# Counting edges in a graph kernel: one-hots of two chunks in one comparison, a span of 24 targets per pair of chunks, 1200 columns of folding per group

## The chip, the cores and the metric

The kernel runs on one core of one Trainium2 chip. The metric is the device time of one execution in microseconds; the median of three runs before the change is 589.65 us (589.12 to 589.82). A profile is one execution recorded by the hardware profiler.

## The reference

Input is `x` (1024 nodes x 512), and 32768 edges `src`, `dst`, sorted by `dst`. Four layers follow each other, each with a residual and a layer norm:

```python
edge_index = jnp.stack([src, dst])
x = _layernorm(x + L0(x, edge_index, W0, b0))            # adj @ (x @ W0), symmetric 0/1 adjacency, normalised
x = _layernorm(x + L1(x, edge_index, W1, b1, W2, b2, W3, b3))   # three GCN convolutions with edge counts
x = _layernorm(x + L2(x, edge_index, Wq, bq, Wk, bk, Wv, bv))   # softmax((q k^T / sqrt d) masked by adj) @ v
x = _layernorm(x + L3(x, edge_index, V1, c1, V2, c2))    # two GCN convolutions, relu between
```

Every layer needs the edges as a dense 1024 x 1024 matrix: how many edges lead from source s to target d. The kernel calls it `count`; the change is wholly in how `count` is made.

## The kernel before, in words

**Counting.** The edges lie in 64 groups (`G`) of 512, a group in 4 chunks (`CPG`) of 128 edges, one edge per partition. A source s is split into low part `s % 128` and high part `s // 128` (8 values). For every chunk two one-hot matrices are made in bf16: `hot_lo` (128 edges x 128 low parts) and `hot_key` (128 edges x 320 keys). A key is the pair of high part (8) and distance of the target from the group's lowest target (`WIN` = 40): 8 x 40 = 320 (`KEYS`). One matmul per chunk, `hot_lo` as weights and `hot_key` as the moving operand (`chunk`, L527), adds the four chunks of a group in one PSUM bank; VectorE adds that bank to 40 columns of each of the 8 blocks of `count` (`add_window`, L1032), at a column that it reads into a register from `base_at` (`windows_at`, L1025, once for 8 groups). Edges are sorted by target, so 512 of them span few targets; how many rounds are needed to cover the widest group is computed on the chip (`rounds`, L1014). In this input the widest group spans 33 targets, so there is one round; pairs of chunks (256 edges) span 18 targets at most.

**Who makes the one-hots.** VectorE makes `hot_lo` of the first two chunks (`BY_DVE` = 2, L1020) and all four `hot_key` (L1022), each by a `tensor_scalar` that compares a 16-bit table of numbers with one fp32 scalar per partition. ScalarE makes `hot_lo` of the other two (L850, L854), and copies the results of the folding (below) out of PSUM. There are 4 slots; VectorE makes the one-hots of group g + 3 (`AHEAD`) before it adds the window of group g. Before an add it waits for two things: `win_summed` (the matmuls of this group) and `win_added` (its own add before). One loop body (`dve.Fori`, L1053) holds 8 groups.

**Folding.** Between groups TensorE is given other work: transposes and products of weights ("pieces", L446 to L509: `xw`, `m`, `u`, `tb`, `w12`, `bw`, `wf`, `g`). A written-out plan spreads them: each group gets a credit of `SHARE` = 1300 columns, and a piece of fp32 with 512 columns counts 1024. What the plan leaves over stands behind the loop: first `BEHIND`, then `REST`, whose first piece waits for `counted` (L454, the whole of `count` is done), and whose pieces stand two by two between the eight transposes of the 0/1 matrix (`turn_links`, L560, L574 to L581). Then come the last piece `g` (L489) and layer 0's aggregation (`rows_step`, L583, L599). With 1300 the plan puts 162 pieces along the loop and 14 behind it, with 1200 it puts 154 along and 22 behind.

**Behind the loop** VectorE makes `link` (L1075, 8 instructions), then one row block of `sym` after each transpose (L1080), with the low parts of the operands of layer 0 between them (`low`, L1066, L1084).

Each engine executes its queue in order. Instructions that only compute a register, load one (`TENSOR_LOAD`), branch or wait are executed by the engine's own sequencer, which can be some instructions ahead of the engine's datapath. The profile calls VectorE's sequencer DVEq.

Of the kernel before, what the change touches and what calls it, by code (L numbers as in the profile page):

```python
# [16 lines left out]
ALU = mybir.AluOpType  # L17
ACT = mybir.ActivationFunctionType
# [8 lines left out]
P = 128  # L27
# [4 lines left out]
CPG = 4  # L32
WIN = 40
BY_DVE = 2
EARLY = 24 * 128
SHARE = 1300
# [7 lines left out]
def gnn_kernel(nc, x, src, dst, w0, b0, w1, b1, w2, b2, w3, b3, wq, bq, wk, bk, wv, bv, v1, c1, v2, c2, out):  # L44
# [7 lines left out]
    KEYS = NB * WIN  # L52
    SCALE = float(D) ** -0.5
    assert N + 2 * WIN <= APART and NB * APART <= 32768
    assert D == 512 and NB == 2 * HALF and G % BODY == 0 and BODY % SLOTS == 0 and KEYS <= 512 and G <= P

    with ExitStack() as ctx:
# [24 lines left out]
        hot_lo = at("hot_lo", at_adj, [P, SLOTS * CPG, P], BF16)  # L82
        hot_key = at("hot_key", at_adj + SLOTS * CPG * P * 2, [P, SLOTS * CPG, KEYS], BF16)
# [41 lines left out]
        keyed = at("keyed", r3 + 2 * W, [P, 3, CPG * G], F32)  # L125
# [32 lines left out]
        col_key = sb("col_key", [P, KEYS], I16)  # L158
# [4 lines left out]
        group_lim = sb("group_lim", [G, 4], F32)  # L163
        group_dia = sb("group_dia", [G, 2, G], F32)
        group_row = sb("group_row", [P, 2, G], F32)
        base_at = sb("base_at", [1, G], I32)
# [40 lines left out]
        win_added = sem("win_added")  # L207
        counted = sem("counted")
# [158 lines left out]
        def _(pool):  # L367
# [17 lines left out]
            nc.gpsimd.iota(col_key[:], pattern=[[APART, NB], [1, WIN]], base=0, channel_multiplier=0,  # L385
# [59 lines left out]
        def _(pe):  # L445
# [78 lines left out]
            pe.matmul(bank[:, 0, 0:2 * G], ones[0:G, :], group_dia[:].rearrange("g a b -> g (a b)"),  # L524
                      start=True, stop=True).then_inc(rows_turned, 1)
# [21 lines left out]
            with pe.If(rounds > 1):  # L547
                with pe.Fori(1, rounds) as r:
                    with pe.Fori(0, G // BODY) as q:
                        for n in range(BODY):  # L550
                            pe.wait_ge(win_added, r * G + q * BODY + (n + 3 - SLOTS))
                            for c in range(CPG):
                                pe.wait_ge(hot_set, (r * G + q * BODY) * CPG + (n * CPG + c + 1))
                                if c == BY_DVE:
                                    pe.wait_ge(act_hot_set, r * G + q * BODY + (n + 1))
                                mm = chunk((n % SLOTS) * CPG + c, n % SLOTS, c)
# [261 lines left out]
        def _(act):  # L818
# [28 lines left out]
            def low_one_hots(g, slot, before):  # L847
# [6 lines left out]
                nc.scalar.activation(hot_lo[:, slot * CPG + BY_DVE:(slot + 1) * CPG, :], apart[:, slot % 2], ACT.Relu,  # L854
# [120 lines left out]
        def _(dve):  # L975
# [3 lines left out]
            def then(ins):  # L979
# [11 lines left out]
            V.tensor_reduce(group_lim[:, 0:1], edge_rows[:, 0, :], AX.X, ALU.min)  # L991
            then(V.tensor_reduce(group_lim[:, 1:2], edge_rows[:, 0, :], AX.X, ALU.max))
            V.tensor_scalar(key_rows[:, 2, :], edge_rows[:, 0, :], group_lim[:, 0:1], None,
                            ALU.subtract).then_inc(rows_set, 1)
            then(V.tensor_tensor(group_lim[:, 2:3], group_lim[:, 1:2], group_lim[:, 0:1], ALU.subtract))
            dve.wait_ge(const_set, 1)
            V.tensor_scalar(group_dia[:, 0, :], ident[0:G, 0:G], group_lim[:, 0:1], None, ALU.mult)
            V.tensor_scalar(group_dia[:, 1, :], ident[0:G, 0:G], group_lim[:, 2:3], None,
                            ALU.mult).then_inc(rows_set, 1)
# [4 lines left out]
            V.tensor_tensor(keyed[:, 1, :], bank[:, 3, 0:CPG * G], edge_key[:, 1, :], ALU.add).then_inc(win_added, 1)  # L1004
            dve.wait_ge(rows_turned, 4)
            V.tensor_copy(group_row[:].rearrange("p a g -> p (a g)"), bank[:, 0, 0:2 * G]).then_inc(win_added, 1)
# [4 lines left out]
            then(V.tensor_copy(flags[0:1, 0:1], rounds_f[0:1, ROUNDS + 1:ROUNDS + 2]))  # L1011
            V.memset(shift[:], 0.0).then_inc(rounds_set, 1)
# [12 lines left out]
            def windows_at(g):  # L1025

                _, values = nc.values_load_multi_w_load_instructions(
                    base_at[0:1, bass.ds(g, BODY)], engines=[mybir.EngineType.DVE], min_val=0, max_val=N,
                    skip_runtime_bounds_check_because="the table's entries are clamped to [0, N] when it is written")
                return values  # L1030

            def add_window(at_dst, seen, slot):  # L1032
# [3 lines left out]
                V.tensor_tensor(count[:, :, bass.ds(at_dst, WIN)],  # L1036
# [276 lines left out]
```

## Time and profile before

| | us |
|---|---|
| median of three runs | 589.65 |
| the profiled execution's own time | 589.9 |
| its span, first to last instruction | 587.6 |
| granted TensorE clock, mean | 0.999 of full |
| first one-hot to last window added | 11.4 to 122.85 |
| folding left over, transposes of the links, `g` | 122.8 to 142.1 |
| layers 0 to 3 | 142.1 to 587.6 |

PE is TensorE, PEld its weight loads, DVE VectorE, ACT ScalarE, POOL GpSimd. A row of a timeline gives start, duration, engine, line, operation and in brackets the idle time before it with what ended it; instructions of one kind that follow each other are merged (x3), and overlap a little, so from the start of one to the start of the next is what counts for a rate. An fp32 matmul appears as two records.

### The profile page before, as it was taken

How to read it: one execution, taken by the hardware profiler on the slowest of the kernel's cores; microseconds unless marked ns; L12 is line 12 of the kernel's file. 1: busy time of each engine (PE TensorE's matmuls, PEld its weight loads, DVE VectorE, ACT ScalarE, POOL GpSimd, SP SyncE). 2: the span in 40 equal slices, each digit the busy share in tenths (PEclk: the TensorE clock that was granted, in tenths of full speed). 3: DMA queues.
4: the chain of work that ended last, by engine and by line, in shares of the span. 5: the costliest groups of instructions: out<-in, count | busy, mean ns of one | idle time of the engine just before them, and what ended most of it. 6: DMA issues, size and time to landing. Idle time of an engine off the chain costs nothing.

```text
span 587.6 us, 6488 instructions
## 1 busy us (share of the span) xinstructions
PE 575.8 (98%) x2121; PEld 344.8 (59%) x2121; DVE 297.2 (51%) x821; ACT 176.6 (30%) x364; POOL 100.4 (17%) x112
## 2 busy tenths in 40 slices
PE   6999999999999999999999999999999999999996
PEld 4555655555788745888845444444445587458743
DVE  7999899948678034233591103333335430450065
ACT  5988689737011311110002011211114102110200
POOL 2000000017333500000170002033332170000011
PEclk9999999999999999999999999999999999999999
DMA  8624000000100000000040000000000000000012
GB/s 300 221 73 143 1 1 1 2 2 6 31 3 0 1 0 0 1 0 1 9 155 0 1 0 1 0 0 1 0 0 1 1 0 1 0 0 1 0 55 91
DMA packets 9429, 16.19 MB, mean 28 GB/s; under 512 B 1571, under 2 KB 1843, under 8 KB 9398
## 3 DMA queue, kind: packets, MB, share of 16 engines
q1 hardware_dynamic: 9398, 15.75, 8.0%
q8 instruction: 22, 0.36, 0.3%
q14 instruction: 9, 0.07, 0.0%
HBM read 13.64 MB, written 2.11 MB: 27 GB/s over the span
## 4 chain that ended last, share of the span: by engine, by line
PE 97%; DVE 1%; issue 1%; DMA 0%; POOL 0%; POOLq 0%; SPq 0%; DVEq 0%
PE bank L663 18%; PE bank L616 15%; PE bank L599 15%; PE bank L764 9%; PE bank L784 9%; PE bank L528 6%; PE bank L499 5%; PE bank L752 5%; PE bank L507 2%; PE bank L472 2%; PE bank L503 2%; PE bank L774 1%; PE bank L460 1%; PE bank L464 1%; PE bank L485 1%; PE bank L671 1%
## 5 line engine op out<-in xcount | busy, mean ns | idle before, releaser
L411 POOL TENSOR_TENSOR rstd<-veps,mhalf 128x1 f32<-128x1 f32 x32 | 23.5, 733 | 301.3 <-DVE veps L1097 298.5
L1022 DVE TENSOR_SCALAR hot_key<-col_key,keyed 128x320 bf16<-128x320 int16 x256 | 65.5, 299 | 0.0
L764 PE MATMUL bank<-xt,tt 128*128 128x512 f32 x128 | 56.1, 593 | 0.0
L784 PE MATMUL bank<-vv,probt 128*128 128x512 f32 x128 | 56.1, 592 | 0.0
L663 PE MATMUL bank<-v_sb,gt 128*128 128x512 f32 (+1 forms) x136 | 55.3, 567 | 0.0
L616 PE MATMUL bank<-adj,y_hi 128*128 128x512 f32 x128 | 51.8, 405 | 0.0
L616 PE MATMUL bank<-adj,y_lo 128*128 128x512 f32 x128 | 50.2, 392 | 0.0
L528 PEld LDWEIGHTS bank<-hot_key,hot_lo 128*128 128x128 bf16 x256 | 25.0, 98 | 38.8 <-DVE hot_key L1022 17.2
L528 PE MATMUL bank<-hot_key,hot_lo 128*128 128x320 bf16 x256 | 45.4, 300 | 0.0
L850 ACT ACTIVATE apart<-col_lo,edge_key 128x128 bf16<-128x128 int16 x128 | 43.8, 390 | 0.0
L1104 DVE SCALAR_TENSOR_TENSOR xs<-bank,dinv,xs 128x512 f32<-128x512 f32 x23 | 17.0, 748 | 52.0 <-PE bank L663 37.3
L663 PEld LDWEIGHTS bank<-v_sb,gt 128*128 128x128 f32 x136 | 25.9, 190 | 28.7 <-issue 27.7
L784 PEld LDWEIGHTS bank<-vv,probt 128*128 128x128 f32 x128 | 24.2, 190 | 29.6 <-issue 29.6
L764 PEld LDWEIGHTS bank<-xt,tt 128*128 128x128 f32 x128 | 23.9, 190 | 27.7 <-issue 27.7
L1211 DVE SCALAR_TENSOR_TENSOR score<-bank,rr,mask 128x1024 f32<-128x1024 f32 x8 | 10.3, 1283 | 55.5 <-PE bank L764 55.5
L1036 DVE TENSOR_TENSOR count<-bank,count 128x320 f32 x64 | 31.3, 488 | 7.1 <-PE bank L528 7.1
L1020 DVE TENSOR_SCALAR hot_lo<-col_lo,edge_key 128x128 bf16<-128x128 int16 x128 | 31.9, 250 | 2.5 <-issue 2.4
L854 ACT ACTIVATE hot_lo<-apart,ones 128x256 bf16<-128x256 bf16 x64 | 32.5, 508 | 2.1
L499 PE MATMUL bank<-w_sb,x0t 128*128 128x512 f32 x64 | 32.6, 607 | 0.0
L431 POOL TENSOR_SCALAR mask<-count 128x1024 bf16<-128x1024 uint16 x8 | 22.5, 2810 | 52.4 <-DVE peak L1219 52.3
L959 ACT COPY probt<-bank 128x1024 f32<-128x1024 f32 x8 | 8.1, 1013 | 72.7 <-PE bank L774 72.7
L616 PEld LDWEIGHTS bank<-adj,y_hi 128*128 128x128 f32 x128 | 24.0, 188 | 6.6 <-issue 0.5
(176 smaller groups left out, 943.4 us busy)
## 6 DMA issues: line engine op xcount, KB each, us to landing
w_sb<-in_L_gnn_W_dram SPq DMA_DIRECT2D x3, 1024.0 KB, 5.5
xs<-in_x_dram SPq DMA_DIRECT2D x2, 1024.0 KB, 6.8
v_sb<-in_L_gnn_W_dram SPq DMA_DIRECT2D x2, 1024.0 KB, 6.8
out_dram<-xs SPq DMA_DIRECT2D x7, 256.0 KB, 2.0
w_sb<-in_L_gnn_weight_dram SPq DMA_DIRECT2D x4, 256.0 KB, 5.9
wq_sb<-in_L_gnn_Wq_dram SPq DMA_DIRECT2D x1, 1024.0 KB, 10.0
wk_sb<-in_L_gnn_Wk_dram SPq DMA_DIRECT2D x1, 1024.0 KB, 11.6
wv_sb<-in_L_gnn_Wv_dram SPq DMA_DIRECT2D x1, 1024.0 KB, 7.6
```

Source lines behind the costliest of these rows:

```text
L499: mm = pe.matmul(to, x0t[:, k, rows], w0_sb[:, k, :], start=first, stop=last)
L528: return pe.matmul(bank[:, at_bank, 0:KEYS], hot_lo[:, at_hot, :], hot_key[:, at_hot, :], start=c == 0, stop=c == CPG - 1)
L599: mm = pe.matmul(to, m[:, k, j * P:(j + 1) * P], y[part][:, k, :], start=k == 0 and part == 0 and m is mat, stop=k == NB - 1 and part == 1 ...
L616: mm = pe.matmul(to, y[part][:, k, f * P:(f + 1) * P], m[:, k, half], start=k == 0 and part == 0 and m is mat, stop=k == NB - 1 and part = ...
L663: mm = pe.matmul(bank[:, 0 if cols is high_cols else HALF * (s % 2) + b, cols], g(k, j), w[:, k, cols], start=k == 0, stop=k == FB - 1)
L764: mm = pe.matmul(bank[:, 2 * (i % 2) + c, :], tt[:, k, i * P:(i + 1) * P], xt[:, k, c * D:(c + 1) * D], start=k == 0, stop=k == FB - 1)
L784: mm = pe.matmul(bank[:, 6 + i % 2, :], probt[:, i % 2, j, :], vv[:, j, :], start=j == 0, stop=j == NB - 1)
L850: ins = nc.scalar.activation(apart[:, slot % 2, c - BY_DVE, :], col_lo[:], ACT.Abs, scale=-1.0, bias=edge_key[:, 0, bass.ds(g + c * G, 1)])
L854: nc.scalar.activation(hot_lo[:, slot * CPG + BY_DVE:(slot + 1) * CPG, :], apart[:, slot % 2], ACT.Relu, scale=-1.0, bias=ones[:, 0:1]).th ...
L1020: V.tensor_scalar(hot_lo[:, slot * CPG + c, :], col_lo[:], edge_key[:, 0, bass.ds(g + c * G, 1)], None, ALU.is_equal)
L1022: V.tensor_scalar(hot_key[:, slot * CPG + c, :], col_key[:], keyed[:, 0, bass.ds(g + c * G, 1)], None, ALU.is_equal).then_inc(hot_set, 1)
L1036: V.tensor_tensor(count[:, :, bass.ds(at_dst, WIN)], bank[:, slot, 0:KEYS].rearrange("p (h d) -> p h d", h=NB), count[:, :, bass.ds(at_dst ...
```

## The change

- The window of a group becomes two spans: chunks 0, 1 and chunks 2, 3 (`PAIR` = 2, `SPANS` = 2) each have their own lowest target and 24 targets (`WIN` = 24, `KEYS` = 192). Both lie beside each other in the group's PSUM bank; each matmul has 192 columns, and VectorE adds two spans of 192 in place of one window of 320.
- VectorE makes one-hots of two chunks by one `tensor_tensor` comparison: the table holds each number twice, side by side (`col_near`, `col_key`), and the other operand, the 16-bit keys of two edges (`lo16`, `key16`), is repeated over it. The two one-hots come out interleaved, so the matmul reads each at a step of two elements. Per group: one `lo_near` (256 elements) and two `hot_key` (384 elements each).
- The order in VectorE's loop changes: wait for the sum, add span 0, make the one-hots of group g + 3, wait for span 0's add (`span_added`), add span 1.
- The places of the two spans are read by two loads of 4 values each, every 4 groups, in place of one load of 8 every 8 groups.
- `SHARE` is 1200. The first `low` stands one step earlier. Setup: minima and maxima per span, four `group_dia`, one more copy (`lo16`), larger iotas.

```diff
-WIN = 40
+WIN = 24
+PAIR = 2
-SHARE = 1300
+SHARE = 1200
+    SPANS = CPG // PAIR
...
-            def chunk(at_hot, at_bank, c):
-                return pe.matmul(bank[:, at_bank, 0:KEYS], hot_lo[:, at_hot, :], hot_key[:, at_hot, :],
-                                 start=c == 0, stop=c == CPG - 1)
+            def chunk(slot, c):
+                span = slice(c // PAIR * KEYS, (c // PAIR + 1) * KEYS)
+                lo = lo_near[:, slot, :, c] if c < BY_DVE else lo_far[:, slot, c - BY_DVE, :]
+                return pe.matmul(bank[:, slot, span], lo, hot_key[:, slot, c // PAIR, :, c % PAIR],
+                                 start=c % PAIR == 0, stop=c % PAIR == PAIR - 1)
...
-            def one_hots(g, slot, chunks=range(CPG)):
-                for c in chunks:
-                    if c < BY_DVE:
-                        V.tensor_scalar(hot_lo[:, slot * CPG + c, :], col_lo[:],
-                                        edge_key[:, 0, bass.ds(g + c * G, 1)], None, ALU.is_equal)
-                    V.tensor_scalar(hot_key[:, slot * CPG + c, :], col_key[:],
-                                    keyed[:, 0, bass.ds(g + c * G, 1)], None, ALU.is_equal).then_inc(hot_set, 1)
+            def one_hots(g, slot):
+                V.tensor_tensor(lo_near[:, slot], col_near[:],
+                                lo16[:, bass.ds(g, 1), :].to_broadcast([P, P, BY_DVE]), ALU.is_equal)
+                for n in range(SPANS):
+                    V.tensor_tensor(hot_key[:, slot, n], col_key[:],
+                                    key16[:, bass.ds(g, 1), n * PAIR:(n + 1) * PAIR].to_broadcast([P, KEYS, PAIR]),
+                                    ALU.is_equal).then_inc(hot_set, 1)
...
+            def places_at(g):
+                loaded = []
+                for n in range(SPANS):
+                    _, values = nc.values_load_multi_w_load_instructions(
+                        base_at[0:1, bass.ds(g + n * G, HALF)], engines=[mybir.EngineType.DVE], min_val=0, max_val=N,
...
+            def add_span(at_dst, slot, n):
+                return V.tensor_tensor(count[:, :, bass.ds(at_dst, WIN)],
+                                       bank[:, slot, n * KEYS:(n + 1) * KEYS].rearrange("p (h d) -> p h d", h=NB),
+                                       count[:, :, bass.ds(at_dst, WIN)], ALU.add)
+
+            def one_group(g, at_dst, seen, slot, ahead):
                 dve.wait_ge(win_summed, seen + 1)
                 dve.wait_ge(win_added, seen + 2)
-                V.tensor_tensor(count[:, :, bass.ds(at_dst, WIN)],
-                                bank[:, slot, 0:KEYS].rearrange("p (h d) -> p h d", h=NB),
-                                count[:, :, bass.ds(at_dst, WIN)], ALU.add).then_inc(win_added, 1)
+                add_span(at_dst[0], slot, 0).then_inc(span_added, 1)
+                if ahead is not None:
+                    one_hots(ahead, (slot + AHEAD) % SLOTS)
+                dve.wait_ge(span_added, seen + 1)
+                add_span(at_dst[1], slot, 1).then_inc(win_added, 1)
...
                 with dve.Fori(0, G // BODY - 1) as q:
-                    places = windows_at(q * BODY)
                     for n in range(BODY):
-                        one_hots(q * BODY + (n + AHEAD), (n + AHEAD) % SLOTS)
-                        add_window(places[n], r * G + q * BODY + n, n % SLOTS)
+                        if n % HALF == 0:
+                            places = places_at(q * BODY + n)
+                        one_group(q * BODY + n, places[n % HALF], r * G + q * BODY + n, n % SLOTS, q * BODY + (n + AHEAD))
...
-                if 3 <= h < 3 + HALF:
-                    low(h - 3, ya, xw[:, h - 3, :], dinv[:, 0, h - 3:h - 2])
+                if 2 <= h < 2 + HALF:
+                    low(h - 2, ya, xw[:, h - 2, :], dinv[:, 0, h - 2:h - 1])
```

## Rows read from the trace of the kernel before

**Rows 1.** The page: busy time by engine, and the chain's shares by engine.

```profile
PE 575.8 (98%) x2121; PEld 344.8 (59%) x2121; DVE 297.2 (51%) x821; ACT 176.6 (30%) x364; POOL 100.4 (17%) x112
PE 97%; DVE 1%; issue 1%; DMA 0%; POOL 0%; POOLq 0%; SPq 0%; DVEq 0%
```

**Rows 2.** Busy time in the loop and in the stretch behind it.

```profile
11.30:122.80 111.50, 111.50 (x532) 63.75 (x530) 101.89 (x449) 88.54 (x230) 0.21 (x1) 1.00 0.21 70
122.80:142.05 19.25, 18.82 (x101) 8.94 (x100) 13.78 (x28) 12.60 (x18) 9.02 (x19) 1.00 0.01 1
```

**Rows 3.** Timeline of VectorE, a group's cycle and an end of the loop body.

```profile
38.10 0.49 DVE L1036 TENSOR_TENSOR count<-bank,count 128x320 f32 x1
38.50 0.25 DVE L1020 TENSOR_SCALAR hot_lo<-col_lo,edge_key 128x128 bf16<-128x128 int16 x1
38.66 0.30 DVE L1022 TENSOR_SCALAR hot_key<-col_key,keyed 128x320 bf16<-128x320 int16 x1
38.87 0.25 DVE L1020 TENSOR_SCALAR hot_lo<-col_lo,edge_key 128x128 bf16<-128x128 int16 x1
39.67 0.49 DVE L1036 TENSOR_TENSOR count<-bank,count 128x320 f32 x1
40.84 0.25 DVE L1020 TENSOR_SCALAR hot_lo<-col_lo,edge_key 128x128 bf16<-128x128 int16 x1 [0.68 <-issue]
```

**Rows 4.** By line: VectorE's instructions and its sequencer's (DVEq), ns min/median/max.

```profile
L1036 DVEq FUSED_REGOPS  x64: 46/53/53, 15.0 to 122.3; - x64
L1036 DVE TENSOR_TENSOR count<-bank,count x64: 479/489/500, 16.1 to 122.4; 128x320 f32 x64
L1027 DVEq TENSOR_LOAD <-base_at x8: 595/598/629, 12.9 to 107.8; - x8
L1014 DVEq TENSOR_LOAD <-flags x1: 553/553/553, 9.4 to 9.4; - x1
L1090 DVE TENSOR_TENSOR xs<-xs,bias x8: 675/946/954, 146.6 to 152.7; 128x512 f32<-128x512 f32 x8
```

**Rows 5.** Timeline of VectorE: instructions that wait for the one before; first one-hot.

```profile
10.52 0.35 DVE L1047 TENSOR_SCALAR keyed<-keyed,shift 128x256 f32<-128x256 f32 x1 [1.12 <-issue]
10.91 0.24 DVE L1048 TENSOR_SCALAR base_at<-group_row,shift 1x64 int32<-1x64 f32 x1
11.37 0.26 DVE L1020 TENSOR_SCALAR hot_lo<-col_lo,edge_key 128x128 bf16<-128x128 int16 x1
```

**Rows 6.** Timeline of TensorE in and behind the loop.

```profile
7.96 3.67 PE L460 MATMUL bank<-ident,xs 128*128 128x128 f32 x16
111.74 0.71 PE L528 MATMUL bank<-hot_key,hot_lo 128*128 128x320 bf16 x4
112.28 1.02 PE L503 MATMUL bank<-w1t,w_sb 128*128 128x512 f32 x2
113.14 0.71 PE L528 MATMUL bank<-hot_key,hot_lo 128*128 128x320 bf16 x4
115.09 0.95 PE L494 MATMUL bank<-bcol,w_sb 128*128 128x1 f32 x8
115.90 1.10 PE L507 MATMUL bank<-w_sb,w12t 128*128 128x512 f32 x2
127.16 0.61 PE L570 MATMUL bank<-identb,link 128*128 128x128 bf16 x8
127.60 1.94 PE L507 MATMUL bank<-w_sb,w12t 128*128 128x512 f32 x4
138.52 3.60 PE L489 MATMUL bank<-w_sb,gcol 128*2 128x512 f32 x8
142.05 0.50 PE L599 MATMUL bank<-ya_hi,sym 128*128 128x512 f32 x1
142.38 0.39 PE L599 MATMUL bank<-ya_lo,sym 128*128 128x512 f32 x1
142.61 0.39 PE L599 MATMUL bank<-ya_hi,sym 128*128 128x512 f32 x1
```

**Rows 7.** Waits of the loop: who for whom, us in total, times, longest.

```profile
PEld bank L528 <- DVE hot_key L1022: 17.2, 51, 0.7
DVE count L1036 <- PE bank L528: 7.1, 8, 1.8
DVE hot_lo L1020 <- issue: 2.4, 4, 0.7
```

**Rows 8.** Timeline of VectorE behind the loop.

```profile
122.36 0.49 DVE L1036 TENSOR_TENSOR count<-bank,count 128x320 f32 x1 [1.80 <-PE bank L528]
123.23 2.43 DVE L1075 TENSOR_SCALAR link<-count 128x1024 bf16<-128x1024 uint16 x7
```

More of the change, by code:

```diff
@@ L81, in gnn_kernel @@
         adj = at("adj", at_adj, [P, NB, N], F32R)
-        hot_lo = at("hot_lo", at_adj, [P, SLOTS * CPG, P], BF16)
-        hot_key = at("hot_key", at_adj + SLOTS * CPG * P * 2, [P, SLOTS * CPG, KEYS], BF16)
+        lo_near = at("lo_near", at_adj, [P, SLOTS, P, BY_DVE], BF16)
+        lo_far = at("lo_far", at_adj + SLOTS * BY_DVE * P * 2, [P, SLOTS, CPG - BY_DVE, P], BF16)
+        hot_key = at("hot_key", at_adj + SLOTS * CPG * P * 2, [P, SLOTS, SPANS, KEYS, PAIR], BF16)
         count = sb("count", [P, NB, N + WIN], U16)
@@ L207, in gnn_kernel @@
         win_added = sem("win_added")
+        span_added = sem("span_added")
         counted = sem("counted")
@@ L853, in low_one_hots @@
                 act.wait_ge(apart_set, before + 1)
-                nc.scalar.activation(hot_lo[:, slot * CPG + BY_DVE:(slot + 1) * CPG, :], apart[:, slot % 2], ACT.Relu,
+                nc.scalar.activation(lo_far[:, slot], apart[:, slot % 2], ACT.Relu,
                                      scale=-1.0, bias=ones[:, 0:1]).then_inc(act_hot_set, 1)
@@ L990, in _ @@
                             ALU.arith_shift_right).then_inc(bits_set, 1)
[L991 to L995, printed above, removed]
+            by_span = edge_rows[:, 0, :].rearrange("g (s e) -> g s e", s=SPANS)
+            V.tensor_reduce(group_lim[:, 0, :], by_span, AX.X, ALU.min)
+            then(V.tensor_reduce(group_lim[:, 1, :], by_span, AX.X, ALU.max))
+            for n in range(SPANS):
+                of_span = slice(n * PAIR * P, (n + 1) * PAIR * P)
+                ins = V.tensor_scalar(key_rows[:, 2, of_span], edge_rows[:, 0, of_span], group_lim[:, 0, n:n + 1], None,
+                                      ALU.subtract)
+            ins.then_inc(rows_set, 1)
+            then(V.tensor_tensor(group_lim[:, 2, :], group_lim[:, 1, :], group_lim[:, 0, :], ALU.subtract))
             dve.wait_ge(const_set, 1)
-            V.tensor_scalar(group_dia[:, 0, :], ident[0:G, 0:G], group_lim[:, 0:1], None, ALU.mult)
-            V.tensor_scalar(group_dia[:, 1, :], ident[0:G, 0:G], group_lim[:, 2:3], None,
-                            ALU.mult).then_inc(rows_set, 1)
+            for n in range(2 * SPANS):
+                ins = V.tensor_scalar(group_dia[:, n, :], ident[0:G, 0:G],
+                                      group_lim[:, 2 * (n // SPANS), n % SPANS:n % SPANS + 1], None, ALU.mult)
+            ins.then_inc(rows_set, 1)
             dve.wait_ge(const_set, 2)
@@ L1003, in _ @@
             dve.wait_ge(edge_set, 1)
-            V.tensor_tensor(keyed[:, 1, :], bank[:, 3, 0:CPG * G], edge_key[:, 1, :], ALU.add).then_inc(win_added, 1)
+            V.tensor_tensor(keyed[:], bank[:, 3, 0:CPG * G], edge_key[:, 1, :], ALU.add).then_inc(win_added, 1)
             dve.wait_ge(rows_turned, 4)
-            V.tensor_copy(group_row[:].rearrange("p a g -> p (a g)"), bank[:, 0, 0:2 * G]).then_inc(win_added, 1)
+            V.tensor_copy(group_row[:].rearrange("p a g -> p (a g)"), bank[:, 0, 0:2 * SPANS * G]).then_inc(win_added, 1)
             dve.wait_ge(win_added, 2)
@@ L1011, in _ @@
             then(V.tensor_copy(flags[0:1, 0:1], rounds_f[0:1, ROUNDS + 1:ROUNDS + 2]))
+            then(V.tensor_copy(lo16[:].rearrange("p g c -> p c g"),
+                               edge_key[:, 0, 0:BY_DVE * G].rearrange("p (c g) -> p c g", c=BY_DVE)))
             V.memset(shift[:], 0.0).then_inc(rounds_set, 1)
@@ L1025, in windows_at @@
[L1025 to L1032, printed above, removed]
+            def one_hots(g, slot):
[5 more added lines that the diff above has]
+                                    ALU.is_equal).then_inc(hot_set, 1)
@@ new lines, in places_at @@
+            def places_at(g):
+                loaded = []
+                for n in range(SPANS):
+                    _, values = nc.values_load_multi_w_load_instructions(
+                        base_at[0:1, bass.ds(g + n * G, HALF)], engines=[mybir.EngineType.DVE], min_val=0, max_val=N,
+                        skip_runtime_bounds_check_because="the table's entries are clamped to [0, N] when it is written")
+                    loaded.append(values)
+                return list(zip(*loaded))
```

43 lines of the change are left out of this document (25 added, 18 removed).

## The prediction, made before the changed kernel was run

> **What bounds the kernel now.** I read the page first: TensorE is busy 98% of the span and 97% of the chain that ended last is its own [rows 1]. Then the two stretches that the change touches [rows 2]: in the loop (11.3 to 122.8 us) TensorE is never idle by the records and VectorE works 101.9 of 111.5 us, so both are near their limit. The waits say the same [rows 7]: weight loads waited 17.2 us for `hot_key`, VectorE 7.1 us for sums. The loop is a balance of two engines; whichever becomes the slower sets its end, and everything behind it follows on TensorE without a gap.
>
> **TensorE's side.** Four chunks take 112.28 - 111.74 = 0.54 us, 0.136 each, then a piece 0.86 us (113.14 - 112.28) [rows 6]. 192 columns for 320 is 0.082 us per chunk if the rate stays: 256 x 0.054 = 13.8 us of TensorE's time saved. Does the step of two bf16 elements slow it? The fp32r matmuls of layer 0 stream 512 columns lying 4 bytes apart in 0.23 us (142.38 to 142.61) [rows 6], about twice the columns per us of fp32 and with the same 4 bytes from column to column as the interleaved bf16; I take no slowdown. The other end is half the rate, 0.163 us per chunk, 64 x 0.32 = 20.5 us more. What 1200 moves: 8 pieces go behind the loop, five of 0.86 (two `w12`, three `wf`) and three `bw` of 0.81 (115.90 - 115.09) [rows 6] = 6.7 us. So TensorE has 114.8 (8.0 to 122.8 [rows 6]) - 13.8 - 6.7 = about 94 us to do up to the loop's end, and could be there at 102.3.
>
> **VectorE's side, the instructions.** Before, a group is 39.67 - 38.10 = 1.57 us [rows 3]: add 0.40 (38.10 to 38.50), two `hot_lo` at 0.16 (38.50 to 38.66), four `hot_key` at 0.21 (38.66 to 38.87). From 128 to 320 columns costs 0.05 us, 0.26 ns per column, so a `hot_key` is 0.083 of streaming and 0.13 fixed; the add streams 320 fp32 at 1.04 ns = 0.333 and has 0.067 fixed; its whole record is 0.155 longer than its stream [rows 3, 4]. The new comparison has two 16-bit inputs, which no row shows. Lower bound of its streaming: 0.26 ns per element as now; upper: 1.04 as the adds. The one-source comparison reads 2 bytes per element in 0.26 ns; two sources read 4, so I take 0.52. Its fixed part: 0.067 as the other `tensor_tensor`, because the 0.13 belongs to a form with a scalar per partition and the SBUF `tensor_tensor` L1090, at its shortest 675 ns for 533 of stream [rows 4], carries no more overhead than the add; upper bound 0.13. So `lo_near` 0.133 + 0.067 = 0.20, a `hot_key` pair 0.20 + 0.067 = 0.27, an add of 192 also 0.20 + 0.067 = 0.27. Sum 0.20 + 4 x 0.27 = 1.28 us: 0.29 less than before, 18.6 us over 64 groups.
>
> The Trainium skill, "VectorE: DVE Perf Modes", section on the perf-mode tier table, says that `tensor_tensor` can take two elements per cycle of 16-bit data and never four, where `tensor_scalar` takes four. That speaks against the change; by it a pair streams in 0.20 us, what I have taken, and the sum stays. No row here shows it.
>
> **VectorE's side, the new order.** Now every group ends with add 1 and the next begins with add 0, and between them stands the wait on `win_added`, which needs add 1 finished. Before, six one-hots stood in front of each add, so this wait cost nothing: the sequencer handled the first add's register at 15.0, the add ran at 16.1 [rows 4], 1.1 us later. With nothing queued between, the start of add 0 lies behind the end of add 1's record (0.20 + 0.155 = 0.355), a wait of 0.04 (10.52 + 0.35 to 10.91 [rows 5]), the register instruction for the address (0.053 [rows 4]) and its dispatch, about 0.05: 0.495 from start to start in place of 0.27. Cycle: 0.27 + 0.20 + 2 x 0.27 + 0.495 = 1.51 us. The wait on `span_added` costs nothing: 0.74 us of one-hots lie in front of it (without them, in the last three groups, 0.31).
>
> **The loads.** One load of 8 values takes 0.598 us of the sequencer, one of one value 0.553 [rows 4]; it is the same for 4, bounds 0.55 and 0.60. Before there were 8, mostly hidden: idle without a releaser is 2.4 us in 4 places [rows 7]; where the sequencer had no lead, at an end of the loop body, the engine stood 1.17 - 0.40 = 0.77 us (39.67 to 40.84 [rows 3]). After there are 32, in 16 pairs, and each pair stands between add 1 and the wait for it. Behind it the engine has at most the one-hots and add 1 of this group: the sequencer gives out add 1 about 0.6 us into the cycle (add 0 finished at 0.355 + 0.04, then two register instructions and the dispatch), loads until 0.6 + 2 x 0.6 + three register instructions of 0.12 = 2.16, and add 0 of the next group starts at 2.35 where it would at 1.51: 0.84 us of standing still, 1.14 where the loop's branch comes too (estimate 0.3 from that 0.77, which is load, branch and address together). 8 x 0.84 + 7 x 1.14 = 14.7 us; the first pair is hidden behind the first three sets of one-hots. Bounds: 0, if the two overlap or run ahead, and 18.
>
> **The sum.** First one-hot at 11.4 [rows 5] plus 0.6 of setup (two more `group_dia`, one more copy, longer rows; 0 to 1.2) = 12.0. Three sets of 0.74: first add at 14.2. 61 cycles x 1.51 = 92.1, loads 14.7, last three groups without one-hots 3.1: the last span is added at 124.1, against 122.85 before [rows 8]. So the loop isn't shorter at all, and TensorE stands about 20 us in it. Then, on TensorE: `counted` 0.2, REST[:4] (two `bw`, two `wf`) 3.3, eight transposes of 0.44 (127.16 to 127.60) = 3.5, the other 16 pieces 2 x 0.81 + 14 x 0.86 = 13.7, `g` 3.5 [rows 6] = 24.2: layer 0 begins at 148.3 in place of 142.1, +6.2 us, nearly all of it the moved pieces. VectorE's `link` (2.8 with the first [rows 8]) is covered by REST[:4], the `sym` blocks by two pieces each. The moved `low` and ScalarE's wait for `bw` stay under this cover; without it `low` is 0.7 us. Behind 142.1 nothing changes. Profiled execution: 589.9 + 6.2 = 596.1; it lies 0.25 above the median of the runs, so those would be at 595.9 us.
>
> **Rivals.**
> 1. The loads hide (they overlap, or the sequencer runs further ahead). For: before, most of the 8 did [rows 7]. Against: those had four to six one-hots queued behind no wait. Then the loop ends at 109.4, layer 0 begins 8.5 us early: 581.2 us. If the add-to-add wait were free too, the cycle is 1.28 and TensorE's 102.3 plus 24.2 and `BEHIND`'s 1.7 sets the start (128.2), with up to 2 us of idle time: 576 to 578.
> 2. The comparison streams one element per 1.04 ns, because of the repeated operand: slower still. `lo_near` 0.33, pairs 0.47, cycle 2.04; the load stalls shrink to 6.8 us (more is queued). Three sets 3.8, 61 x 2.04 = 124.4, 3.1: end at 150.1, 26 us more than forecast, 622 us. From 1.75 us per group, stalls in, the change loses; this mechanism alone passes it. Against: the innermost run is two adjacent elements, and the one-source form keeps 0.26 ns per element on 16-bit data [rows 3]; no row has a repeated operand. The Trainium skill, "Vector Engine (DVE) Microarchitecture Reference", section 5.1, reports that a row read over and over with a step of 0 still ran two elements per cycle with two sources, and a single element repeated ran one; by that rule this rival falls. No row here shows either.
> 3. TensorE reads the interleaved operands at half rate. With VectorE as bound its 20.5 us disappear in the 20 us of idle time: 596 to 597. Only together with rival 1 does it decide: then the gain of that rival is gone.
> 4. The rounds. If a pair spanned 24 or more targets, a second round would repeat the loop, +100 us; the widest pair spans 18 here, chance zero.
>
> **How the numbers follow.** Forecast 0.52; rival 1 at 581 with its neighbours (part of the stalls hidden) 0.28, its faster form 0.06; rival 2 0.07; between them, within 0.2% of before, 0.07. (0.2% is about what a measurement of this kernel can tell from no change.) Faster 0.34, same 0.07, slower 0.59. The forecast's own range is 591 to 605: 605 with a fixed part of 0.13 (cycle 1.70, stalls 11.8: +9), 591 with loads at a third less. The range that holds 8 in 10 adds rival 1: 580 to 605.
>
> **What would show it.** In the profile after: about 0.35 us records of `hot_key` with starts 0.27 apart (0.47: rival 2); add 0 beginning 0.5 behind add 1; idle time of VectorE before add 0 with releaser "issue", 15 times, 0.8 to 1.2 us; weight loads waiting some 20 us or more for `hot_key`; chunks starting 0.083 apart; the last add near 124. A cycle under 1.6 us on average, or TensorE never idle in the loop, would make the prediction wrong.

## The result and the profile after

The changed kernel takes 590.6 us (median of 15 runs, 590.21 to 591.34) against 589.6 us of the kernel before (589.12 to 589.82): ratio 1.0019, 95% interval 1.0011 to 1.0027. That is +1.0 us where +6.2 was forecast. The profiled execution spans 588.5 us against 587.6.

The page of the kernel after, busy time and shares of the chain (the answer to [rows 1]), and its two stretches (the answer to [rows 2]):

```profile
PE 569.0 (97%) x2121; PEld 336.8 (57%) x2121; DVE 283.0 (48%) x697; ACT 176.2 (30%) x364; POOL 97.2 (17%) x113
PE 89%; DVE 5%; issue 3%; DVEq 1%; ACT 1%; DMA 1%; POOL 0%; POOLq 0%; SPq 0%
```

```profile
11.30:117.20 105.90, 99.91 (x503) 53.32 (x501) 89.02 (x329) 89.35 (x231) 0.20 (x1) 1.00 0.21 73
117.20:143.10 25.90, 25.17 (x137) 13.45 (x136) 14.98 (x29) 12.91 (x19) 14.32 (x32) 1.00 0.00 1
```

The loop ends 5.7 us earlier (117.2 for 122.85) and the stretch behind it is 6.6 us longer (25.9 for 19.25), so layer 0 begins 1.07 us later. TensorE, never idle in the loop before, is now idle for 6 of 105.9 us: the loop has become VectorE's, and the chain shows it (DVE 5% and issue 3%, for 1% and 1%).

Timeline of VectorE after: a group's cycle, an end of the loop body, and the middle of a body (answers to [rows 3]).

```profile
35.74 0.36 DVE L1057 TENSOR_TENSOR count<-bank,count 128x192 f32 x1 [0.34 <-DVE count L1057]
39.02 0.28 DVE L1038 TENSOR_TENSOR lo_near<-col_near,lo 128x256 bf16<-128x256 int16 x1
39.22 0.62 DVE L1041 TENSOR_TENSOR hot_key<-col_key,key 128x384 bf16<-128x384 int16 x2
39.75 0.86 DVE L1057 TENSOR_TENSOR count<-bank,count 128x192 f32 x2
40.52 0.28 DVE L1038 TENSOR_TENSOR lo_near<-col_near,lo 128x256 bf16<-128x256 int16 x1
41.26 0.35 DVE L1057 TENSOR_TENSOR count<-bank,count 128x192 f32 x1
42.50 0.36 DVE L1057 TENSOR_TENSOR count<-bank,count 128x192 f32 x1 [0.89 <-PE bank L539]
```

The cycle is 40.52 - 39.02 = 1.50 us (forecast 1.51): `lo_near` 0.20, two `hot_key` 0.53, then two adds, of which the second starts 0.5 us behind the first. In the middle of a body the first add of the next group comes 0.2 us later than that (35.74); at the end of a body the adds are 42.50 - 41.26 = 1.24 us apart, 0.75 more than the usual 0.5. With these stalls in, the 61 cycles take 1.60 us on average, just at the limit below which the prediction called itself wrong. The trace names TensorE's sum or VectorE's own add before, now one and now the other, but such stalls stand only where places are loaded (but for one of 0.16 us before the second group), and they are gone in the kernel without loads (below): what comes last there is the sequencer. By line (the answers to [rows 4]):

```profile
L1049 DVEq TENSOR_LOAD <-base_at x32: 340/342/378, 14.5 to 112.2; - x32
L1057 DVE TENSOR_TENSOR count<-bank,count x128: 350/357/363, 16.3 to 116.8; 128x192 f32 x128
```

A load of 4 values takes 0.342 us, where 8 took 0.598 and 1 took 0.553 [rows 4].

The setup, VectorE, GpSimd (POOL) and TensorE after (the first one-hot answers to [rows 5]); `bits` of the kernel before follows in a fence of its own:

```profile
2.25 0.76 POOL L392 IOTA col_near<- 128x256 int16 x1
2.97 1.14 POOL L394 IOTA col_key<- 128x384 int16 x1
4.14 1.41 POOL L398 MEMSET count<- 128x1572 f32 x1
4.40 1.42 DVE L1001 TENSOR_SCALAR bits<-edge_rows 64x512 int32<-64x512 int32 x1 [0.82 <-DMA edge_rows<-in_src_dram]
8.87 1.22 PE L533 MATMUL bank<-group_dia,ones 64*128 64x256 f32 x2 [0.15 <-DVE group_dia L1015]
10.13 0.42 DVE L1024 COPY group_row<-bank 128x256 f32<-128x256 f32 x1 [0.89 <-PE bank L533]
14.12 0.29 DVE L1038 TENSOR_TENSOR lo_near<-col_near,lo 128x256 bf16<-128x256 int16 x1
```

```profile
4.21 0.42 DVE L988 TENSOR_SCALAR bits<-edge_rows 64x512 int32<-64x512 int32 x1 [0.59 <-DMA edge_rows<-in_src_dram]
7.23 0.79 PE L524 MATMUL bank<-group_dia,ones 64*128 64x128 f32 x2
```

The same `bits` took 0.42 us before and takes 1.42 now, beside GpSimd's memset, which the two larger iotas have pushed to 4.14. The first one-hot starts at 14.12 in place of 11.37.

TensorE after, in and behind the loop (answers to [rows 6]), and the waits (answers to [rows 7]):

```profile
112.90 0.34 PE L539 MATMUL bank<-hot_key,lo_near 128*128 128x192 bf16 x2
113.08 0.33 PE L539 MATMUL bank<-hot_key,lo_far 128*128 128x192 bf16 x2
113.25 1.04 PE L512 MATMUL bank<-w1t,w_sb 128*128 128x512 f32 x2
139.60 3.59 PE L498 MATMUL bank<-w_sb,gcol 128*2 128x512 f32 x8 [0.68 <-ACT wfold L857]
143.12 0.50 PE L612 MATMUL bank<-ya_hi,sym 128*128 128x512 f32 x1
```

```profile
PEld bank L539 <- issue: 42.0, 91, 1.4
DVE count L1057 <- PE bank L539: 5.4, 11, 0.9
```

Four chunks take 113.25 - 112.90 = 0.35 us, 0.088 each, so the step of two elements doesn't slow TensorE to half rate (0.163). Its weight loads wait 42 us, nearly always without a releaser in the trace; for `hot_key` the trace names 0.7 us, where the prediction expected 20 or more as a sign.

### The profile page after: what moved, and what is told of

Same layout as the page of the kernel before. It is cut to its first block, busy times and chain, and to the rows that moved or that the text cites. A ratio compares the mean times of both kernels' runs of the same rounds, so it can differ in the third digit from the quotient of the medians.

```text
span 588.5 us, 6305 instructions
## 1 busy us (share of the span) xinstructions
PE 569.0 (97%) x2121; PEld 336.8 (57%) x2121; DVE 283.0 (48%) x697; ACT 176.2 (30%) x364; POOL 97.2 (17%) x113
## 4 chain that ended last, share of the span: by engine, by line
PE 89%; DVE 5%; issue 3%; DVEq 1%; ACT 1%; DMA 1%; POOL 0%; POOLq 0%; SPq 0%
PE bank L676 18%; PE bank L629 15%; PE bank L612 15%; PE bank L777 9%; PE bank L797 9%; PE bank L765 5%; PE bank L539 3%; PE bank L516 2%; PE bank L481 2%; PE bank L508 2%; DVE hot_key L1041 2%; PE bank L512 2%; DVE count L1057 1%; PE bank L787 1%; PE bank L494 1%
## 5 line engine op out<-in xcount | busy, mean ns | idle before, releaser
L1057 DVE TENSOR_TENSOR count<-bank,count 128x192 f32 x128 | 45.6, 356 | 15.5 <-PE bank L539 5.4
L797 PEld LDWEIGHTS bank<-vv,probt 128*128 128x128 f32 x128 | 24.2, 190 | 29.7 <-issue 29.7
L1041 DVE TENSOR_TENSOR hot_key<-col_key,key 128x384 bf16<-128x384 int16 x128 | 39.8, 352 | 0.0
L539 PEld LDWEIGHTS bank<-hot_key,lo_near 128*128 128x128 bf16 x128 | 10.8, 97 | 42.7 <-issue 41.2
L867 ACT ACTIVATE lo_far<-apart,ones 128x256 bf16<-128x256 bf16 x64 | 32.7, 511 | 2.1
L676 PE MATMUL bank<-wv_sb,xt 128*128 128x512 f32 x64 | 27.8, 592 | 0.0
L765 PE MATMUL bank<-xt,mfold 128*128 128x512 f32 x64 | 27.8, 592 | 0.0
L676 PE MATMUL bank<-wfold,gt 128*128 128x512 f32 x64 | 27.6, 592 | 0.0
```

Source lines behind the costliest of these rows:

```text
L539: return pe.matmul(bank[:, slot, span], lo, hot_key[:, slot, c // PAIR, :, c % PAIR], start=c % PAIR == 0, stop=c % PAIR == PAIR - 1)
L676: mm = pe.matmul(bank[:, 0 if cols is high_cols else HALF * (s % 2) + b, cols], g(k, j), w[:, k, cols], start=k == 0, stop=k == FB - 1)
L765: mm = pe.matmul(bank[:, HALF * (s % 2) + f, :], mfold[:, k, f * P:(f + 1) * P], xt[:, k, half * D:(half + 1) * D], start=k == 0, stop=k = ...
L797: mm = pe.matmul(bank[:, 6 + i % 2, :], probt[:, i % 2, j, :], vv[:, j, :], start=j == 0, stop=j == NB - 1)
L867: nc.scalar.activation(lo_far[:, slot], apart[:, slot % 2], ACT.Relu, scale=-1.0, bias=ones[:, 0:1]).then_inc(act_hot_set, 1)
L1041: V.tensor_tensor(hot_key[:, slot, n], col_key[:], key16[:, bass.ds(g, 1), n * PAIR:(n + 1) * PAIR].to_broadcast([P, KEYS, PAIR]), ALU.is_ ...
```

## The experiments

All are compared with the kernel before, run on the same chip (589.3 to 589.5 us). Theory A: the loop is VectorE's; its length is the 1.50 us cycle, in which the add-to-add wait stands, plus the stalls by the loads (short ones), and work moved between loop and the stretch behind is paid where it stands. "Layer 0" is the start of its first matmul: 142.05 before, 143.12 after.

### What moving 8 pieces is worth in the kernel before

```diff
-SHARE = 1300
+SHARE = 1200
```

> The kernel before with one part of the change alone: SHARE 1200, so 8 pieces (6.7 us of TensorE) stand behind the loop in place of in it. Theory A (before, both engines were the bound of the loop, so pieces taken out of it shorten it by about what they cost behind it): the loop ends near 116, layer 0 still begins at 142 +- 1, time 589 to 591 us. Rival B (what is moved behind the loop is paid in full whatever the loop's bound): 595 to 596 us.

589.9 us, ratio 1.0009 (1.0000 to 1.0019). The loop ends at 115.9, 6.9 us earlier, and layer 0 begins at 142.5. So the move alone is free in the kernel before, whose loop is TensorE's. It also gives the right kernel to compare with: at the same 1200 columns the change makes the loop not 5.7 us shorter but 1.3 us longer (117.2 for 115.9). One load in this loop shows a stall, behind two waits for sums:

```profile
79.49 0.26 DVE L1020 TENSOR_SCALAR hot_lo<-col_lo,edge_key 128x128 bf16<-128x128 int16 x1 [0.57 <-issue]
```

### 1400 columns in the changed kernel

```diff
-SHARE = 1200
+SHARE = 1400
```

> The changed kernel with SHARE 1400. Theory A (in the changed loop VectorE is the bound by its cycle of 1.50 us and the load stalls, and TensorE stands idle some 14 us, so folding put back into the loop is free): the loop still ends near 118, the stretch behind it is 12 us shorter, time 579 to 582 us. Rival B (TensorE is held by its own reading of interleaved operands or its waits per chunk, so the loop grows with what is put in): 589 to 591 us.

587.1 us, ratio 0.9962 (0.9948 to 0.9976). The loop takes TensorE's idle 6 us and ends 3.1 us later, at 120.3; but layer 0 begins only 3.4 us earlier, at 139.76. TensorE behind the loop, and its clock (column before the last two) in that stretch:

```profile
127.12 0.62 PE L583 MATMUL bank<-identb,link 128*128 128x128 bf16 x8 [0.54 <-DVE sym L1111]
131.48 1.03 PE L583 MATMUL bank<-identb,link 128*128 128x128 bf16 x8 [1.45 <-DVE sym L1111]
134.25 5.58 PE L498 MATMUL bank<-w_sb,gcol 128*2 128x512 f32 x8
```

```profile
126.00:131.00 5.00, 2.44 (x35) 1.75 (x32) 5.00 (x8) 4.68 (x6) 3.60 (x9) 1.00 0.00 0
131.00:134.20 3.20, 1.95 (x16) 1.54 (x16) 3.20 (x7) 3.19 (x5) 2.88 (x7) 0.57 0.00 0
134.20:139.80 5.60, 5.60 (x11) 0.81 (x9) 3.79 (x7) 1.25 (x2) 5.19 (x12) 0.64 0.00 0
```

The pieces were the cover of VectorE's `sym` blocks. Without them the transposes wait for `sym` (five times, 3.8 us), TensorE is busy 2.44 of 5.0 us, its granted clock falls to 0.57, near the lower of its two levels (1.2 GHz), and `g` takes 5.58 us instead of 3.59. Both costs together are most of what is missing.

### The two iotas behind GpSimd's memset

```diff
-            nc.gpsimd.iota(col_near[:], ...)
-            nc.gpsimd.iota(col_key[:], ...)
             nc.gpsimd.memset(mhalf[:], -0.5)
...
             nc.gpsimd.memset(count[:, ZEROED:NB, :].bitcast(F32), 0.0).then_inc(const_set, 1)
+            nc.gpsimd.iota(col_near[:], ...)
+            nc.gpsimd.iota(col_key[:], ...).then_inc(const_set, 1)
```

> The changed kernel with GpSimd's two long iotas (0.76 and 1.14 us) put behind its memset of count. Theory A (VectorE's first comparison of the edges took 1.42 us in place of 0.42 because GpSimd's memset of count now runs beside it and the two share a way to memory): that row is back at 0.42, one-hots begin about 1 us earlier, 589.3 to 590 us. Rival B (any GpSimd write holds VectorE, the iotas as well): the row stays long or another one grows, 590.6 us or more.

590.4 us, ratio 1.0016 (1.0006 to 1.0025): no better. GpSimd and VectorE in its setup:

```profile
4.10 0.61 DVE L1001 TENSOR_SCALAR bits<-edge_rows 64x512 int32<-64x512 int32 x1 [0.52 <-DMA edge_rows<-in_src_dram]
4.39 1.25 POOL L397 IOTA col_key<- 128x384 int16 x1
4.63 1.28 DVE L1002 TENSOR_SCALAR bits<-edge_rows 64x512 int32<-64x512 int32 x1
```

The delay moved to the next `bits` (1.28 for 0.41, and 0.61 for 0.42 in the first). An iota holds this instruction up as the memset did, and in both kernels the long `bits` ends 0.27 us after GpSimd's write (5.82 and 5.55; 5.91 and 5.64). Not every instruction of VectorE is held: in the kernel with both edits (below) a copy from PSUM beside the same iota takes its usual 0.42 us.

```profile
8.39 1.15 POOL L398 IOTA col_key<- 128x384 int16 x1
8.91 0.42 DVE L1025 COPY group_row<-bank 128x256 f32<-128x256 f32 x1 [0.89 <-PE bank L534]
```

### The second pair's one-hots behind the second add

```diff
                 if ahead is not None:
-                    one_hots(ahead, (slot + AHEAD) % SLOTS)
+                    one_hots(ahead, (slot + AHEAD) % SLOTS, [0])
                 dve.wait_ge(span_added, seen + 1)
                 add_span(at_dst[1], slot, 1).then_inc(win_added, 1)
+                if ahead is not None:
+                    one_hots(ahead, (slot + AHEAD) % SLOTS, [1])
```

> The changed kernel with the one-hots of pair 1 moved behind the add of span 1, so that something is queued between this add and the next group's add, which waits for it. Theory A (this wait costs 0.22 us per group): VectorE's cycle falls from 1.50 to 1.28 us, the loop ends 7 to 9 us earlier, 582 to 584 us. Rival B (TensorE's sums are what VectorE really waits for): cycle unchanged in the mean, 590 us.

583.9 us, ratio 0.9911 (0.9895 to 0.9928). VectorE in its loop:

```profile
30.10 0.28 DVE L1039 TENSOR_TENSOR lo_near<-col_near,lo 128x256 bf16<-128x256 int16 x1
30.30 0.35 DVE L1042 TENSOR_TENSOR hot_key<-col_key,key 128x384 bf16<-128x384 int16 x1
30.57 0.35 DVE L1058 TENSOR_TENSOR count<-bank,count 128x192 f32 x1
30.84 0.34 DVE L1042 TENSOR_TENSOR hot_key<-col_key,key 128x384 bf16<-128x384 int16 x1
31.10 0.34 DVE L1058 TENSOR_TENSOR count<-bank,count 128x192 f32 x1
31.37 0.28 DVE L1039 TENSOR_TENSOR lo_near<-col_near,lo 128x256 bf16<-128x256 int16 x1
```

The same instructions in 1.27 us instead of 1.50: a one-hot stands in front of each add and covers the wait for the add before. The loop ends at 110.2, 7.0 us earlier, where 61 cycles would give 14.0. Most of the rest is in the cycles with loads:

```profile
34.13 0.36 DVE L1058 TENSOR_TENSOR count<-bank,count 128x192 f32 x1 [0.42 <-issue]
63.96 0.36 DVE L1058 TENSOR_TENSOR count<-bank,count 128x192 f32 x1 [0.96 <-issue]
```

From `lo_near` to `lo_near`, a cycle in the middle of a body is 1.77 us (1.71 without the split) and one at its end 2.32 (2.25): these 14 cycles gained nothing, 4.7 us less than 14 x 0.23 would be. So it is not the engine's own work that sets them; in the kernel with one element repeated (below), whose cycle is 2.03, the middles show no stall at all and the ends are again 2.25. The three kernels together point at the sequencer's chain of loads and registers, which takes 1.7 to 1.8 us in a middle cycle and some 2.3 at an end; no run takes this chain apart. The other part is waits for TensorE's sums, in four or five cycles of 1.4 to 2.1 us: TensorE is busy 93.6 of 96.2 us. The split without the loads was not run.

### No loads

The places of the spans are constants, 16 columns per group; the counts thus land at other targets, and the loads are left out.

```diff
-                loaded = []
...
-                return list(zip(*loaded))
+                return [((g + n) * 16, (g + n) * 16 + 8) for n in range(HALF)]
```

> The changed kernel without the 32 loads of places: spans are added at columns computed from the group's number (16 g and 16 g + 8), so the counts lie at other targets than the reference's. Theory A (the loads cost VectorE 0.20 us at each of 8 places and 0.75 us, with the branch, at 7 ends of the loop body, 6.9 us in all, and VectorE is the bound): every cycle 1.50 us, loop ends near 110.5, time 583 to 585 us. Rival B (the branch is the larger part of it): 587 to 588.5 us.

584.8 us, ratio 0.9919 (0.9903 to 0.9936); the loop ends at 110.7. The stalls in the middle and at the end of bodies are gone, and the loop is 6.5 us shorter, the whole 5.8, where the prediction had 14.7 for the loads. The edit does a little more than take them out: in the last eight groups, which stand behind the loop body, the columns are now constants, and two adds start 0.40 us apart instead of 0.50.

```profile
103.80 0.74 DVE L1051 TENSOR_TENSOR count<-bank,count 128x192 uint16<-128x192 f32 x2
```

That gives about 1.1 us, and new waits for sums (0.25 us, twice) and other small ones take nearly as much. So 6.5 us is near the 6.3 us of stalls counted in the trace, but isn't a clean measurement of them.

### One load of 8 values

```diff
-                loaded = []
-                for n in range(SPANS):
-                    ...(base_at[0:1, bass.ds(g + n * G, HALF)], ...)
+                _, values = ...(base_at[0:1, bass.ds(g * SPANS, HALF * SPANS)], ...)
+                return [values[SPANS * n:SPANS * (n + 1)] for n in range(HALF)]
```

> The changed kernel with the places of both spans side by side, so that one load of 8 values stands in place of two of 4. Theory A (a load's length goes with its values: 0.34 us for 4, 0.60 for 8, so one of 8 is 0.6 and two of 4 are 0.34 + 0.13 + 0.34 = 0.8): stall 0.02 and 0.55 us in place of 0.20 and 0.75, together 3 us less, 587 to 588.5 us. Rival B (the 0.60 before was something else than the number of values, and 8 cost 0.35 too): 585 to 586 us.

590.9 us, ratio 1.0026 (1.0010 to 1.0043), with runs from 588.9 to 592.9: the time is inconclusive. The profiled execution (588.88 us) has

```profile
L1047 DVEq TENSOR_LOAD <-base_at x16: 594/599/630, 14.4 to 110.3; - x16
42.35 0.36 DVE L1054 TENSOR_TENSOR count<-bank,count 128x192 f32 x1 [0.68 <-DVE count L1054]
```

The first line is a group by line, the second from the timeline. Eight values are 0.6 us again, in this kernel too, and the stalls shrink: none in the middle of a body (0.20 before), and 0.54 for 0.75 at its end, with 0.12 more in the cycle after it. That is 4.2 us of stalls for 6.3; a longer first wait for TensorE takes 0.7 back, and the loop ends at 115.8, 1.4 us earlier. So two loads of 4 (0.68) cost a little more than one of 8 (0.60). The five runs of about 592 us have a mean granted clock of 0.991 to 0.994, the five of about 589 (median 589.25) one of 0.997 to 1.0. Only a short one was profiled, so where the clock fell in the long ones, and why, stays open.

### One element repeated instead of a pair

The one-hots are not interleaved: the table holds the numbers once per chunk, and each key is repeated alone over the innermost run. TensorE then reads adjacent elements.

```diff
-        hot_key = at(..., [P, SLOTS, SPANS, KEYS, PAIR], BF16)
+        hot_key = at(..., [P, SLOTS, SPANS, PAIR, KEYS], BF16)
...
-                                    key16[...].to_broadcast([P, KEYS, PAIR]),
+                                    key16[...].rearrange("p o c -> p c o").to_broadcast([P, PAIR, KEYS]),
```

> The changed kernel with the one-hots of two chunks one behind the other in place of interleaved: the same comparison with the same number of elements, but its second operand now is one element repeated along the innermost run. Theory A (two 16-bit elements per step need a pair of adjacent elements in every operand): lo_near 0.33 us and hot_key 0.47 us from start to start in place of 0.20 and 0.27, cycle 2.03 us, loop 28 to 30 us longer, 617 to 621 us. Rival B (the interleave isn't what gives the rate): 590.6 us.

620.1 us (two runs), ratio 1.052 (1.0487 to 1.0554). VectorE in its loop:

```profile
29.68 1.02 DVE L1041 TENSOR_TENSOR hot_key<-col_key,key 128x384 bf16<-128x384 int16 x2
30.61 0.85 DVE L1057 TENSOR_TENSOR count<-bank,count 128x192 f32 x2
```

The cycle is 2.03 us. Two comparisons take 0.93 us instead of 0.53: 0.47 each, which less 0.067 is 1.04 ns per element, twice the price of the interleaved form. This is rival 2 of the prediction, nearly to its 622 us, and it shows what the interleaving by two is for. Its sign on the stalls was right too: with a cycle of 2.03 only six ends of a body show one, of 0.2 us. And it settles rival 3: TensorE reads adjacent elements here, and a chunk's record is 0.243 us in the median for 0.247 interleaved, its weight load 0.096 for 0.097.

### Both together: split one-hots, and the iotas behind `rows_set`

To the split is added that GpSimd writes the two tables only when VectorE is through with the rows (`pool.wait_ge(rows_set, 2)` ahead of the iotas, which stand behind the memset).

> The changed kernel with pair 1's one-hots behind the add of span 1, and GpSimd's two long iotas started only when VectorE has written group_dia, with its memset of count in front of them. Theory A (GpSimd's writes beside VectorE's first comparisons of the edges cost 1.0 us; now none runs there): bits rows at 0.42 us both, first one-hot near 13, 582.5 to 583.3 us, 0.9 us under the split alone (583.9). Rival B (the start is set by TensorE's wider matmul and its wait): 583.9 us.

582.6 us, ratio 0.9884 (0.9868 to 0.9901), 1.3 us better than the split alone. Both `bits` take 0.42 us again and the first one-hot stands at 12.90, 1.22 us earlier.

### Short loads in the kernel before

```diff
-                    base_at[0:1, bass.ds(g, BODY)], ...
+                    base_at[0:1, bass.ds(g, BODY // 2)], ...
...
                     for n in range(BODY):
+                        if n % 4 == 0:
+                            places = windows_at(q * BODY + n)
```

> The kernel before, with one edit: each load of 8 window places at the top of a body becomes two loads of 4, one at the top and one before the fifth group. It tests the step of the prediction that failed, the price of a short load, in the other kernel. Theory A (a load's length goes with the number of values: 0.34 us for 4, 0.60 for 8, as the profile after and the kernel with one load of 8 show): the stall at a body's top falls from 0.68 us to about 0.42 (7 times, 1.8 us), and the load in the middle of a body is hidden by the two or so instructions that VectorE still has under way there; the loop ends 1.8 us earlier and the time is 587.8 us (587.3 to 588.5). Rival B (a load is priced by the trip, 0.60 us whatever it fetches, and what shortened it in the changed kernel was something else): the stall at the top stays at 0.68, the eight extra loads stall 0.1 to 0.2 us each, and the time is 590.5 to 591.5 us.

589.5 us, ratio 1.0005 (0.9996 to 1.0015). By line, and the end of a body in the timeline:

```profile
L1027 DVEq TENSOR_LOAD <-base_at x16: 341/343/383, 12.8 to 114.1; - x16
40.55 0.25 DVE L1020 TENSOR_SCALAR hot_lo<-col_lo,edge_key 128x128 bf16<-128x128 int16 x1 [0.45 <-issue]
```

The price is confirmed: 0.343 us, and the stall falls from 0.68 to 0.45 us [rows 3]; the loads in the middle of bodies cost nothing. The time is neither theory's. Only four of seven ends of bodies show the stall at all; and where adds had come 0.14 us earlier (60.76 for 60.90 in the kernel before), they are back at 64.45 for 64.48 once TensorE's larger pieces set the cycle. What VectorE gains, it gives back at the next wait for a sum.

### More folding in the kernel with both edits

```diff
-SHARE = 1200
+SHARE = 1250
```

> The changed kernel with the second pair's one-hots behind the second add and the two comparison tables written behind GpSimd's memset, and 1250 columns of folding a group instead of 1200. With 1200 the loop of that kernel has TensorE busy for 94.2 of 96.4 us, so its slack is only 2.2 us. Theory A (the stretch is now bound by TensorE's work, wherever it stands): about two and a half pieces, some 2 us, move into the loop; what slack is left takes up to 1 us, the rest lengthens the loop by as much as it shortens the stretch behind: 581.9 us (581.2 to 582.6). Rival B (VectorE still bounds the loop, and every column moved into it is free, as between the two kernels before with 1200 and 1300): 580.6 us or less.

580.7 us, ratio 0.9858 (0.9841 to 0.9874): between the two theories, within 0.1 us of B's bound. The loop ends 1.3 us later (110.6), layer 0 begins 2.5 us earlier (133.05).

> As the kernel with 1250 columns, with 1300. Theory A (TensorE's work is the bound): the loop is full, its end moves by what is moved in, and the time is within 0.7 us of that with 1250: 581.9 us (581.2 to 583). Rival B (free): 579 us or less. Rival C (VectorE's adds now wait for TensorE's sums group by group and it gets longer than what it saves): 583.5 us or more.

579.7 us, ratio 0.9844 (0.9828 to 0.9860), the best kernel of this study. The loop ends at 113.6, 4.3 us later than with 1200, and layer 0 begins at 132.4, 3.1 us earlier. Its two stretches:

```profile
13.00:113.60 100.60, 99.30 (x529) 59.26 (x529) 83.57 (x321) 87.27 (x230) 0.20 (x1) 1.00 0.20 71
113.60:132.40 18.80, 18.36 (x98) 8.67 (x96) 14.36 (x28) 12.35 (x16) 9.37 (x20) 1.00 0.00 1
```

TensorE is busy 99.3 of 100.6 us. The trace puts 15.1 us of VectorE's idle time down to TensorE's sums; about 7 of them stand at places of loads, where the sequencer may be what came last, the other 8 don't. The loop is TensorE's again, as in the kernel before, but it ends 9.2 us earlier than there. The time lies between theories A (581.2 to 583) and B (579 or less); A undersized what slack was left: the last 50 columns gave 0.9 us for 3.0 us of loop.

## Why the prediction was wrong in size

**Cycle of VectorE: right.** 1.50 us for 1.51. The comparison at 0.52 ns per element with 0.067 fixed (0.27 from start to start), the adds at 0.27, and the add-to-add wait of 0.495 in place of 0.27 were all there; the split removed that wait and took 0.23 us off the cycle. The rule of the Trainium skill, "VectorE: DVE Perf Modes", on `tensor_tensor` of 16-bit data holds by this row: 384 elements in 0.20 us are two per cycle of the adds' 1.04 ns. So does what "Vector Engine (DVE) Microarchitecture Reference", section 5.1, reports of operands read at step 0: a single element repeated ran at half that rate, 0.47 us.

**The loads: the step that failed.** "One load of 8 values takes 0.598 us of the sequencer, one of one value 0.553 [rows 4]; it is the same for 4, bounds 0.55 and 0.60." It is 0.342. From the two ends I took a constant, though no row had 4. Measured in the trace: six ends of a body at 0.75 or a little more, seven middles at 0.21 and one more of 0.28 (the last end, which has no branch back) = 6.3 us, in place of 14.7. This is -8.4 us. The mechanism was right (each pair between two adds, with nothing queued behind no wait), its price was not: with 0.342 put into the prediction's own chain, each stall is 0.51 us less, 0.33 and 0.63, and the sum 8 x 0.33 + 7 x 0.63 = 7.0 us. What is left are smaller errors: the branch adds 0.54 us at an end and not 0.3, a middle costs 0.21 and not 0.33, and the load before the last four groups shows no stall. The loads did not hide, as rival 1 had it; they were short.

**Setup: sized too small.** 2.75 us for 0.6 (bounds 0 to 1.2). 1.22 us of it are the iotas: the kernel with both edits, which keeps them away from `bits`, has its first one-hot at 12.90; I had counted them as "larger iotas" with no cost since GpSimd has nothing behind them, and overlooked that its memset would then run beside `bits`. Of the other 1.5 us, 0.76 are the matmul of `group_dia` over 256 columns (1.22 for 0.79): the copy of `group_row` now waits for it and starts 1.3 us behind `keyed`, where it was 0.55. The rest are the copy `lo16` (0.3), the longer copy of `group_row` (0.42 for 0.29) and `key` in 16 bits (0.51 for 0.35), and smaller ones.

**The loop's end.** 124.1 forecast; + 2.1 (first one-hot at 14.12 for 12.0) - 8.4 (loads) - 0.6 (61 cycles) + 0.2 (a first wait for TensorE) - 0.3 (last three groups 2.8 for 3.1) = 117.1; measured 117.13.

**Behind the loop: nearly right.** 25.9 for 24.2: the 20 pieces and eight transposes take 21.4 us for 20.5 (two pieces between transposes 1.77 to 1.81 for 1.67 to 1.72), and `g` waits 0.68 us for ScalarE's last copy of `wfold`, a wait I had put under cover. Sum: -7.0 + 1.7 = -5.3; forecast +6.2, so +0.9, measured +1.07 at layer 0 and +1.0 in the medians.

**The direction: luck.** With only the loads priced as they are, the same sum gives 589.9 + 6.2 - 8.4, less than before: faster. That the kernel still came out 1.0 us slower, as forecast, is owed to the setup and the stretch behind the loop, both undersized.

**TensorE and the moved pieces: right.** Chunks at 0.088 for 0.082, no rival 3; 8 pieces cost some 7 us behind the loop, and with a loop of VectorE they bring nothing in it. At equal columns the change as it stands loses: 4.3 us saved by the shorter cycle (60 x 0.07; 0.29 less of instructions, 0.22 more of add-to-add wait), 1.7 us of waits gone (1.1 for TensorE's sums, 0.6 at a load), against 6.3 us of load stalls, with a first add 0.25 us later; that is +0.6 of the 1.3 us, and the rest, in the first and the last groups, I have not taken apart.

## What to carry to other kernels

When one long wait is split into two dependent steps, put independent work in front of both, not of one: the order of one instruction was worth 6.7 us here, more than what was left of the cheaper instructions without it (4.3 us). Price a sequencer's load by a row with that many values, and look at how much work is queued behind no wait where it stands: the 14 cycles with loads gained nothing when the engine's own work in them became shorter. After the bound has moved to the other engine, choose the amount of moved work anew, and stop where the work that covers the next chain (here `sym`) would run out.

## What the runs showed of the hardware that was not expected

- `TENSOR_LOAD` on VectorE's sequencer: 0.342 us for 4 values (in the changed kernel, and 0.343 in the kernel before with short loads), 0.598 for 8 (in two), 0.553 for one from another tile [rows 4]. It does not grow evenly with the number of values.
- VectorE's `tensor_scalar` on 32-bit rows in SBUF takes 1.42 us instead of 0.42 beside a memset of GpSimd, 1.28 beside an iota, and ends 0.27 us after GpSimd's write in both; a copy from PSUM beside an iota keeps its 0.42.
- In the changed kernel with 1400 columns TensorE had four gaps of 0.5 to 1.5 us between bursts of eight matmuls (126 to 131.5 us), and its granted clock was 0.57 in the mean from 131.0 to 134.2; in the kernel with both edits and 1300 columns, which has one gap of 0.43 us there, it stayed at 1.00.
- A cycle of VectorE with a pair of short loads took 1.71 us in the middle of a body and 2.25 at its end where the other cycles took 1.50, and 1.77 and 2.32 where they took 1.27.
